# Third block of the key operand: copied on chip by ScalarE instead of loaded a third time

## The chip, the cores and the metric

The kernel runs on one core of a Trainium2 chip. The metric is the device time of one execution in microseconds; the time before is the median of three runs.

## The reference

A batch of 8 sequences of 224 rows of 512 features passes a cross attention over 750 context rows with 16 heads of 32 features, and then a feed-forward part that picks the 2 nearest of 32 prototypes for each row. Shortened:

```python
q, k, v = layernorm(x) @ w_q.T + b_q, ctx @ w_k.T + b_k, ctx @ w_v.T + b_v   # 16 heads of 32
scores = einsum('bthd,bshd->bhts', q * 32 ** -0.5, k) + bias[None]
scores = where(mask[:, None, None, :], NEG_INF, scores)
x = x + einsum('bhts,bshd->bthd', softmax(scores), v).reshape(8, 224, 512) @ w_o.T + b_o
y = layernorm(x)
w = softmax(-distance(y, prototypes) / t);  topw, topi = top_k(w, 2)         # topw made to sum to 1
x = x + sum over the two slots of topw * (A[topi] @ (B[topi] @ y) + bias[topi])
```

## The kernel before, in words

Everything is computed in 32-bit floats. To keep precision, a projection splits each operand in a high part (rounded to the fp32r format, in which TensorE multiplies) and a low part (the rest), and adds up three products: high by high, high by low, low by high.

The first stage (`weave`) does the attention. Its work is cut in 256 units: unit `w` is one head and one half of the 224 query rows of one batch. 32 units make a batch, 8 units a group of four heads (a group is numbered `n`, 0 to 31; four groups make a batch). While TensorE does the units of batch b, it also does the projections of batch b+1 in small shares between the steps of a unit (`project_steps`). In the last batch, units 224 to 255, there is nothing left to project. Before unit 0 the projections of batch 0 run alone.

Projected keys and queries go from the chip to memory (`k_parts`, `q_parts`, each with a high and a low part) and come back in another layout (`load_keys`, line 351). For one group there are four heads side by side in the free dimension, and in the partitions 97 rows: three blocks of 32 features, and a row with the mask (against a row of ones). With `k_st` as the moving operand and `q_st` as the weights, one product over 97 rows gives all three partial products and the mask at once. The blocks are key high, key low, key high, against query high, query high, query low. So the third key block is the same data as the first: it is loaded from memory twice. `k_st` and `q_st` are double buffered by the group's parity.

What the engines do in one unit:

- TensorE, `turn(w, 0)`: three transposes of probabilities (line 867), which wait for the Exp of unit w and for VectorE's copy of the unit before; then some projection steps, `score(w + 2)` (lines 854 and 858), some more, `turn(w, 1)`, and the rest. After every fourth unit comes `weigh` (line 885), the product with the values `v_sb`, and after every eighth the transposes of the sums (line 894).
- VectorE: the addition of the bias with the row maximum (line 696), the copy of half of the transposed probabilities (line 706), the low parts of projection tiles (lines 639, 646, 652) and, once a group, the product `attn` (line 720).
- ScalarE: the Exp of unit w+1 (line 574), the high parts of projection tiles (lines 553, 561, 568), the copy of the other half of the probabilities (line 583) and, once a group in its third unit, `sums_out` (line 589), which releases line 720.

Each engine works off its own list, written out by hand, in order; a wait holds up all that stands behind it. In the fourth unit of batches 1 to 6 TensorE's transposes also wait for line 720 of the group before (line 914), as the transposes of the next batch's `x` use the same bank.

SyncE issues the transfers, also in order: the stores of finished projection tiles (`store_tile`), the key load of group n+2 in the seventh unit of group n (line 425), the value load of a group in its second unit (line 427, line 376), and the context loads in halves. In the last batch GpSimd issues the loads of the weights for the second stage (line 481). Value tiles use two buffers: a tile waits for the store of the one two before.

The second stage (`finish`) begins after the last unit, about 770 us into the span. It does the output projection and the feed-forward part.

Of the kernel before, what the change touches and what calls it, by code (L numbers as in the profile page):

```python
# [8 lines left out]
F32 = mybir.dt.float32  # L9
# [3 lines left out]
ACT = mybir.ActivationFunctionType  # L13
AX = mybir.AxisListType

P = 128
B, T, E = 8, 224, 512
S = 750
H, D = 16, 32
NP, RK = 32, 16  # L20
KT = E // P
HG = P // D
NG = H // HG
# [6 lines left out]
UG = HG * TC  # L30
# [48 lines left out]
UNITS = B * UB  # L79
# [58 lines left out]
def ended(b, u, *pieces):  # L138

    if b >= B or u < 0:  # L140
        return []
    cuts, ends = CUTS[b][u], tile_ends(b)
    return [n for n in range(NT) for p in pieces if cuts[p] < ends[n] <= cuts[p + 1]]
# [54 lines left out]
def weave(nc, x, ctx_t, bias, mask, w_in_t, b_in, bv, b_out, scratch, attn_t, w_dram, sh):  # L198


    with ExitStack() as ctx:
# [3 lines left out]
        def sem(name):  # L205
            return ctx.enter_context(nc.semaphore(name))
# [95 lines left out]
        exp_done = sem("exp_done")  # L302
        prob_ready = [sem(f"prob_ready{j}") for j in range(2)]
        prob_copied = [sem(f"prob_copied{j}") for j in range(2)]
        weigh_done = sem("weigh_done")
        rsum_ready = sem("rsum_ready")
        rsum_wide_ready = sem("rsum_wide_ready")
# [12 lines left out]
        def _(eng):  # L320
# [30 lines left out]
            def load_keys(n):  # L351
                b, g = divmod(n, NG)
                p = g % 2
                if n >= 2:
                    eng.wait_ge(score_ready, UG * (n - 1))
                eng.wait_ge(k_stored[g], 64 * (b + 1))
                eng.wait_ge(q_stored[g // 2], 32 * (b + 1))
                if g < 2:
                    eng.dma_start(k_st[p][MROW:MROW + 1, :, :].bitcast(F32),
                                  scratch["mask"][b:b + 1, :].unsqueeze(1).broadcast_to([1, HG, S]))\  # L360
                       .then_inc(kq_loaded[p], 16)
                for j in range(NBLK):
                    eng.dma_start(k_st[p][j * D:(j + 1) * D, :, :].bitcast(F32),
                                  scratch["k"][b, (0, 1, 0)[j], g * P:(g + 1) * P, :]
                                  .rearrange("(r d) s -> d r s", d=D)).then_inc(kq_loaded[p], 16)
                    eng.dma_start(q_st[p][j * D:(j + 1) * D, :, :].bitcast(F32),
                                  scratch["q"][b, (0, 0, 1)[j], g * P:(g + 1) * P, :]
                                  .rearrange("(r d) t -> d r t", d=D)).then_inc(kq_loaded[p], 16)
# [174 lines left out]
        def _(eng):  # L543
# [28 lines left out]
            def exp(w):  # L572
                eng.wait_ge(added, w + 1)
                nc.scalar.activation(scores[:, w % NSC, :], scores[:, w % NSC, :], ACT.Exp,  # L574
                                     bias=neg_max[:, w % UB:w % UB + 1], scale=-1.0,
                                     accum_out=sums[:, w % UB:w % UB + 1]).then_inc(exp_done, 1)

            def copy(w):
                q, h = divmod(w, HG)
                if h == 0 and q >= 2:  # L580
# [3 lines left out]
                                     prob_ps[1][0:SW, 0:BT * TW].rearrange("p (s t) -> p s t", s=BT),  # L584
                                     ACT.Copy).then_inc(prob_copied[1], 1)

            def sums_out(n):
                eng.wait_ge(out_ready, n + 1)
                nc.scalar.activation(rsum_t[:, :], out_ps[:, 256:256 + T], ACT.Copy).then_inc(rsum_t_ready, 1)
# [21 lines left out]
                    nc.scalar.activation(w_hi[2][:, k, :], w_stage[2][:, k, :], ACT.Copy).then_inc(wv_hi_ready, 1)  # L611
            eng.wait_ge(wk_ready, KT)
            eng.wait_ge(wv_ready, KT)
            exp(0)
            for w in range(UNITS + 3):
                b, u = divmod(w, UB)
                if w + 1 < UNITS:
                    exp(w + 1)
                for n in ended(b + 1, u - 1, 2) + ended(b + 1, u, 0):
                    high_tile(b + 1, n)  # L620
                if b + 1 < B and u in X_AT:
                    high_x(b + 1, X_AT.index(u), out_ps)
                if w < UNITS:
                    copy(w)
                for n in ended(b + 1, u, 1):
                    high_tile(b + 1, n)
                if u % UG == 2 and w > UG:
                    sums_out(w // UG - 1)
# [160 lines left out]
        def _(eng):  # L789
# [53 lines left out]
            def score(w):  # L843
                n, h, c = w // UG, w % HG, w // HG % TC
                b, g = divmod(n, NG)
                p = n % 2
                if w % UG == 0:
                    eng.wait_ge(kq_loaded[p], 208 * b + 16 + 96 * (g // 2 + 1))
                at = 786 * (w % 2)
                main = (0, 512) if w % 2 == 0 else (S - 512, S)  # L850
                mid = (512, S) if w % 2 == 0 else (0, S - 512)
                if w >= 2:
                    eng.wait_ge(added, w - 1)
                nc.tensor.matmul(score_ps[:, at + main[0]:at + main[1]], q_st[p][:, h, c * TW:(c + 1) * TW],  # L854
                                 k_st[p][:, h, main[0]:main[1]], start=True, stop=True)
                if w >= 1:
                    eng.wait_ge(added, w)
                nc.tensor.matmul(score_ps[:, at + mid[0]:at + mid[1]], q_st[p][:, h, c * TW:(c + 1) * TW],  # L858
                                 k_st[p][:, h, mid[0]:mid[1]], start=True, stop=True).then_inc(score_ready, 1)
# [659 lines left out]
```

## Time and profile before

| | |
|---|---|
| median of 3 runs | 972.43 us (969.31 to 973.49) |
| profiled execution | 967.28 us |
| its span | 965.6 us |
| TensorE products busy | 873.9 us, 91% |
| VectorE busy | 616.2 us, 64% |
| ScalarE busy | 499.7 us, 52% |
| DMA | 144.35 MB, mean 149 GB/s |
| key loads | 96 transfers of 375 KB |

The span is the time from the first to the last instruction that the profiler sees. The percentages are shares of the span, over stages with different limits; so the table says which engine is loaded most, not what is worth how much. PE stands for TensorE's products, PEld for its weight loads, DVE for VectorE, ACT for ScalarE, POOL for GpSimd, SPq for the transfers that SyncE issues.

### The profile page before, as it was taken

Reading aid. Unit: us, or ns where it says so; the run is one execution under the profiler, and the core shown is the slowest. Engines: PE = TensorE matmul, PEld = TensorE weight load, DVE = VectorE, ACT = ScalarE, POOL = GpSimd, SP = SyncE. Lnnn points to the kernel's source line nnn. Section 1 sums busy time; section 2 is a strip of 40 time slices with the busy share of each in tenths; the row PEclk is TensorE's granted clock in tenths of the full one; section 3 lists DMA queues with packets and bytes.
Section 4 is the critical chain, followed back from the end, with each engine's and each line's share of the span. In section 5 each row is a group of like instructions: output and inputs, shape, how many; then the busy total and the mean of one; then the engine's idle time right before and its main releaser. Section 6 shows DMA issues by size and latency. Waiting matters only on the chain. (4 is left out here: it accounts for less than half of the span.)

```text
span 965.6 us, 21000 instructions
## 1 busy us (share of the span) xinstructions
PE 873.9 (91%) x8016; PEld 761.5 (79%) x8016; DVE 616.2 (64%) x1452; ACT 499.7 (52%) x1061; POOL 199.1 (21%) x245
## 2 busy tenths in 40 slices
PE   7577999999999999999999999999948868999996
PEld 6556897898789888978988898889747648888884
DVE  5425677667666766776686667666637556666662
ACT  4204565655556555656655665556537625334441
POOL 2241011212100210112021002110146222234300
PEclk9778999999999999999999999999979979999999
DMA  7585675977577576758775675576585311112201
GB/s 246 177 196 163 169 204 127 216 191 192 125 191 219 147 166 179 203 137 207 189 195 128 184 214 151 144 194 181 132 176 151 93 49 39 57 57 67 67 20 38
DMA packets 107803, 144.35 MB, mean 149 GB/s; under 512 B 8869, under 2 KB 83149, under 8 KB 107714
## 3 DMA queue, kind: packets, MB, share of 16 engines
q1 hardware_dynamic: 105218, 134.49, 54.0%
q0 software_dynamic: 2496, 8.65, 3.1%
q8 instruction: 59, 0.97, 0.5%
q14 instruction: 30, 0.25, 0.1%
HBM read 91.54 MB, written 51.57 MB: 148 GB/s over the span
## 5 line engine op out<-in xcount | busy, mean ns | idle before, releaser
L574 ACT ACTIVATE score_sb<-score_sb,neg_max 112x750 f32<-112x750 f32 x256 | 235.9, 921 | 108.7 <-DVE neg_max L696 107.9
L696 DVE CUSTOM_DVE_ANT_0 score_sb<-score_ps,neg_bias 112x750 f32<-112x750 f32 x256 | 239.4, 935 | 63.5 <-PE score_ps L858 61.8
L867 PE MATMUL prob_ps<-ident,score_sb 112*125 112x112 f32 x1536 | 254.5, 275 | 18.6 <-ACT score_sb L574 8.2
L867 PEld LDWEIGHTS prob_ps<-ident,score_sb 112*125 112x125 f32 x1536 | 226.0, 188 | 51.5 <-issue 13.5
L706 DVE COPY probs_sb<-prob_ps 125x336 f32<-125x336 f32 x256 | 129.6, 506 | 132.6 <-PE prob_ps L867 130.4
L583 ACT ACTIVATE probs_sb<-prob_ps 125x336 f32<-125x336 f32 x256 | 114.8, 448 | 191.9 <-PE prob_ps L867 190.4
L473 POOL COPY rsum_wide<-rsum 112x256 f32<-112x256 f32 x32 | 12.7, 397 | 472.3 <-DVE rsum L715 472.3
L854 PE MATMUL score_ps<-k_st,q_st 97*112 97x512 f32 x256 | 108.2, 423 | 0.0
L813 PE MATMUL acc<-ctx_hi,w_hi 128*128 128x376 f32 (+1 forms) x256 | 92.9, 363 | 14.5 <-DVE k_lo L639 7.8
L885 PE MATMUL out_ps<-probs_sb,v_sb 125*32 125x112 f32 x3072 | 88.0, 263 | 12.7 <-DMA v_sb<-v_all 12.1
L813 PE MATMUL acc<-ctx_hi,w_lo 128*128 128x376 f32 (+1 forms) x256 | 91.0, 355 | 0.0
L885 PEld LDWEIGHTS out_ps<-probs_sb,v_sb 125*32 125x32 f32 x3072 | 72.4, 111 | 23.2 <-DMA v_sb<-v_all 12.4
L813 PE MATMUL acc<-ctx_lo,w_hi 128*128 128x376 f32 (+1 forms) x256 | 90.6, 354 | 0.0
L821 PE MATMUL acc<-w_hi,ctx_hi 128*125 128x512 f32 x192 | 81.6, 425 | 6.6 <-DVE v_out L646 6.6
L858 PE MATMUL score_ps<-k_st,q_st 97*112 97x238 f32 x256 | 72.8, 284 | 10.6 <-DVE neg_max L696 9.9
L821 PE MATMUL acc<-w_hi,ctx_lo 128*125 128x512 f32 x192 | 81.2, 423 | 0.0
L821 PE MATMUL acc<-w_lo,ctx_hi 128*125 128x512 f32 x192 | 79.5, 414 | 0.0
L813 PEld LDWEIGHTS acc<-ctx_hi,w_hi 128*128 128x128 f32 x256 | 49.9, 195 | 18.0 <-DVE k_lo L639 8.3
L858 PEld LDWEIGHTS score_ps<-k_st,q_st 97*112 97x112 f32 x256 | 45.5, 178 | 22.6 <-DVE neg_max L696 18.1
L466 POOL TENSOR_TENSOR ctx_lo<-ctx_raw,ctx_hi 128x376 fp32r<-128x376 f32 x56 | 55.5, 992 | 4.7
L813 PEld LDWEIGHTS acc<-ctx_lo,w_hi 128*128 128x128 f32 x256 | 50.1, 196 | 1.3
L813 PEld LDWEIGHTS acc<-ctx_hi,w_lo 128*128 128x128 f32 x256 | 49.8, 195 | 1.2
(159 smaller groups left out, 1504.0 us busy)
## 6 DMA issues: line engine op xcount, KB each, us to landing
k_st<-k_parts SPq DMA_DIRECT2D x96, 375.0 KB
v_all<-v_out SPq DMA_DIRECT2D x48, 250.0 KB
v_sb<-v_all SPq DMA_DIRECT2D x32, 375.0 KB
q_st<-q_parts SPq DMA_DIRECT2D x96, 112.0 KB
ctx_raw<-in_ctx_t SPq DMA_DIRECT2D x14, 752.0 KB, 7.9
k_parts<-k_hi SPq DMA_DIRECT2D x32, 188.0 KB, 2.4
k_parts<-k_lo SPq DMA_DIRECT2D x32, 188.0 KB, 4.9
k_parts<-k_hi SPq DMA_DIRECT2D x32, 187.0 KB, 3.1
```

The lines of the kernel that those rows point to most:

```text
L466: eng.tensor_tensor(ctx_lo[f][:, k, :], src, ctx_hi[f][:, k, :].bitcast(F32), ALU.subtract)\
L473: eng.tensor_copy(rsum_wide[:, :, :, :], rsum[:, :].rearrange("t (c r) -> t c r", c=TC).unsqueeze(3) .broadcast_to([TW, TC, HG, D])).then_ ...
L574: nc.scalar.activation(scores[:, w % NSC, :], scores[:, w % NSC, :], ACT.Exp, bias=neg_max[:, w % UB:w % UB + 1], scale=-1.0, accum_out=su ...
L583: nc.scalar.activation(probs_sb[q % 2][0:SW, h * ST + BT:(h + 1) * ST, :], prob_ps[1][0:SW, 0:BT * TW].rearrange("p (s t) -> p s t", s=BT) ...
L696: nc.vector.tensor_tensor_reduce(out=scores[:, w % NSC, :], in0=score_ps[:, at:at + S], in1=neg_bias[:, w // HG % TC, :], scale=1.0, scala ...
L706: nc.vector.tensor_copy(probs_sb[q % 2][0:SW, h * ST:h * ST + BT, :], prob_ps[0][0:SW, 0:BT * TW].rearrange("p (s t) -> p s t", s=BT))\
L813: last = nc.tensor.matmul(acc[n % 2][:, 0:SH[f]], w_part[a][1][:, k, g * P:(g + 1) * P], ctx_part[c][f][:, k, K_AT[f]:K_AT[f] + SH[f]], st ...
L821: last = nc.tensor.matmul(acc[n % 2][0:SW, :], ctx_part[c][f][:, k, at:at + SW], w_part[a][2][:, k, :], start=(r == 0), stop=(m == end - 1))
L854: nc.tensor.matmul(score_ps[:, at + main[0]:at + main[1]], q_st[p][:, h, c * TW:(c + 1) * TW], k_st[p][:, h, main[0]:main[1]], start=True, ...
L858: nc.tensor.matmul(score_ps[:, at + mid[0]:at + mid[1]], q_st[p][:, h, c * TW:(c + 1) * TW], k_st[p][:, h, mid[0]:mid[1]], start=True, sto ...
L867: last = nc.tensor.transpose(prob_ps[j][0:SW, s * TW:(s + 1) * TW], scores[:, w % NSC, (BT * j + s) * SW:(BT * j + s + 1) * SW], ident[0:T ...
L885: last = nc.tensor.matmul(out_ps[h * D:(h + 1) * D, c * TW:(c + 1) * TW], v_g[p][:, s, h * D:(h + 1) * D], probs_sb[q % 2][0:SW, h * ST + ...
```

## The change

The third key block is no longer loaded. SyncE issues only the loads of blocks 0 and 1 (the three loads of `q_st` stay), so the counts that are waited for go from 96 to 80 a group pair. ScalarE copies block 0 to block 2, one head at a time: 32 partitions by 750 elements, 128 copies in all. The first copy of a group waits for the group's whole key load. The four copies of group n stand in the third to sixth unit of group n-1, each right behind the copy of line 583 and ahead of `sums_out`. Those of groups 0 and 1 stand ahead of the first Exp. The first score product of a group waits for the load and for its four copies.

```diff
+        k_copied = sem("k_copied")
...
                 for j in range(NBLK):
-                    eng.dma_start(k_st[p][j * D:(j + 1) * D, :, :].bitcast(F32),
-                                  scratch["k"][b, (0, 1, 0)[j], g * P:(g + 1) * P, :]
-                                  .rearrange("(r d) s -> d r s", d=D)).then_inc(kq_loaded[p], 16)
+                    if j < 2:
+                        eng.dma_start(k_st[p][j * D:(j + 1) * D, :, :].bitcast(F32),
+                                      scratch["k"][b, j, g * P:(g + 1) * P, :]
+                                      .rearrange("(r d) s -> d r s", d=D)).then_inc(kq_loaded[p], 16)
...
+            def copy_keys(n, h):
+
+                b, g = divmod(n, NG)
+                p = g % 2
+                if h == 0:
+                    eng.wait_ge(kq_loaded[p], 176 * b + 16 + 80 * (g // 2 + 1))
+                nc.scalar.activation(k_st[p][2 * D:3 * D, h, :], k_st[p][0:D, h, :].bitcast(F32), ACT.Copy)\
+                    .then_inc(k_copied, 1)
...
             eng.wait_ge(wv_ready, KT)
+            for n in range(2):
+                for h in range(HG):
+                    copy_keys(n, h)
             exp(0)
...
                 if w < UNITS:
                     copy(w)
+                if 2 <= u % UG < 2 + HG and UG < w < UNITS - UG:
+                    copy_keys(w // UG + 1, u % UG - 2)
...
                 if w % UG == 0:
-                    eng.wait_ge(kq_loaded[p], 208 * b + 16 + 96 * (g // 2 + 1))
+                    eng.wait_ge(kq_loaded[p], 176 * b + 16 + 80 * (g // 2 + 1))
+                    eng.wait_ge(k_copied, HG * (n + 1))
```

## Rows read from the trace of the kernel before

**Rows 1.** The page's first part: busy time, share and instructions of each engine.

```profile
PE 873.9 (91%) x8016; PEld 761.5 (79%) x8016; DVE 616.2 (64%) x1452; ACT 499.7 (52%) x1061; POOL 199.1 (21%) x245
```

**Rows 2.** Windows: stretch and length, busy of each engine, granted clock, DMA share, GB/s.

```profile
61.00:79.00 18.00, 8.96 (x27) 6.80 (x27) 6.02 (x11) 0.00 (x0) 4.80 (x7) 0.69 0.63 148
168.00:181.00 13.00, 12.07 (x123) 10.94 (x122) 7.51 (x19) 8.41 (x18) 4.79 (x7) 1.00 1.04 221
457.50:480.00 22.50, 22.50 (x240) 20.32 (x239) 14.81 (x34) 13.27 (x29) 2.85 (x4) 1.00 0.72 180
706.00:718.00 12.00, 0.84 (x15) 0.66 (x17) 1.06 (x3) 1.85 (x5) 5.33 (x7) 0.59 1.02 198
725.00:739.60 14.60, 13.11 (x162) 10.51 (x162) 11.51 (x27) 11.30 (x28) 11.61 (x15) 1.00 0.53 136
```

**Rows 3.** Waits from 90 to 700 us: total, times, longest, in us.

```profile
PE prob_ps L867 <- DVE attn L720: 3.6, 6, 0.6
```

**Rows 4.** Timeline of the start: start, duration, instruction, idle before it and releaser.

```profile
75.26 0.69 DVE L646 TENSOR_TENSOR v_out<-acc,bv_row 125x512 f32<-125x512 f32 x1 [7.55 <-DMA v_all<-v_out]
79.21 0.54 PE L858 MATMUL score_ps<-k_st,q_st 97*112 97x238 f32 x1 [5.88 <-DVE neg_max L696]
79.28 0.92 ACT L574 ACTIVATE score_sb<-score_sb,neg_max 112x750 f32<-112x750 f32 x1 [31.93 <-DVE neg_max L696]
```

**Rows 5.** Timeline around 717 us: the value load's issue and the product behind it.

```profile
699.46 0.27 SPq L376 DMA_DIRECT2D v_sb<-v_all  x1
...
717.45 2.47 PE L885 MATMUL out_ps<-probs_sb,v_sb 125*32 125x112 f32 x48 [11.16 <-DMA v_sb<-v_all]
```

**Rows 6.** ScalarE's groups by shape: busy us, mean ns, idle before.

```profile
L574 ACT ACTIVATE score_sb<-score_sb,neg_max 112x750 f32<-112x750 f32 x256 | 235.9, 921 | 108.7 <-DVE neg_max L696 107.9
L593 ACT ACTIVATE w_hi<-probs_sb 128x512 fp32r<-128x512 f32 x4 | 2.5, 630 | 3.1 <-DMA probs_sb<-in_w_in_t 3.0
L595 ACT ACTIVATE ctx_hi<-ctx_raw 128x376 fp32r<-128x376 f32 x4 | 2.1, 514 | 0.1
```

**Rows 7.** Timeline of ScalarE, VectorE and TensorE around 176 and 185 us.

```profile
175.31 0.45 ACT L583 ACTIVATE probs_sb<-prob_ps 125x336 f32<-125x336 f32 x1 [0.70 <-PE prob_ps L867]
175.66 0.35 ACT L589 ACTIVATE rsum_t<-out_ps 128x224 f32<-128x224 f32 x1
176.15 0.38 DVE L720 TENSOR_TENSOR attn<-out_ps,rsum_t 128x224 f32<-128x224 f32 x1
176.58 0.58 PE L867 MATMUL prob_ps<-ident,score_sb 112*125 112x112 f32 x3 [0.60 <-DVE attn L720]
184.62 0.44 ACT L583 ACTIVATE probs_sb<-prob_ps 125x336 f32<-125x336 f32 x1
186.81 0.40 PE L854 MATMUL score_ps<-k_st,q_st 97*112 97x512 f32 x1
```

**Rows 8.** The page's last part: issues with their count and size.

```profile
k_st<-k_parts SPq DMA_DIRECT2D x96, 375.0 KB
v_all<-v_out SPq DMA_DIRECT2D x48, 250.0 KB
...
q_st<-q_parts SPq DMA_DIRECT2D x96, 112.0 KB
```

**Rows 9.** Timeline of SyncE's issues: start and duration of the issue.

```profile
65.88 12.71 SPq L342 DMA_DIRECT2D v_all<-v_out  x4
...
166.08 0.64 SPq L359 DMA_DIRECT2D k_st<-mask_rows  x1
```

**Rows 10.** ScalarE's idle times in one group of the last batch.

```profile
731.57 0.92 ACT L574 ACTIVATE score_sb<-score_sb,neg_max 112x750 f32<-112x750 f32 x1 [0.30 <-DVE neg_max L696]
...
733.09 0.92 ACT L574 ACTIVATE score_sb<-score_sb,neg_max 112x750 f32<-112x750 f32 x1 [0.17 <-DVE neg_max L696]
...
734.69 0.92 ACT L574 ACTIVATE score_sb<-score_sb,neg_max 112x750 f32<-112x750 f32 x1 [0.25 <-DVE neg_max L696]
...
736.37 0.45 ACT L583 ACTIVATE probs_sb<-prob_ps 125x336 f32<-125x336 f32 x1 [0.67 <-PE prob_ps L867]
```

## The prediction

> **What bounds the kernel.** I read the page's totals first: TensorE is busy 873.9 us of 965.6, ScalarE 499.7 [rows 1]. Then the windows: in the long stretch in which one batch's attention is woven with the next batch's projections (about 79 to 694 us), a window such as 457.5 to 480 has TensorE busy all of its 22.5 us with ScalarE busy 13.27; the last batch, which has nothing to project, looks otherwise: in 14.6 us TensorE has 13.1 and ScalarE 11.3 [rows 2]. So whatever makes TensorE wait in the long stretch is lost one for one, and ScalarE work there is free as long as nothing on TensorE waits for it; in the last batch a ScalarE delay soon shows. Third, TensorE's waits: from 90 to 700 us they are small, among them six of 0.6 us each for `attn`, line 720 [rows 3]. Outside that stretch, two stalls come from DMA: at the start (61 to 79 us, TensorE busy 8.96 of 18 at a mean granted clock of 0.69), and 11.16 us for `v_sb` at 717.45 [rows 2, 4, 5]. The change takes from DMA and adds to ScalarE, so it must be priced at these places; the average load of either says nothing.
>
> **Price of one added copy.** 128 instructions of 32 x 750. ScalarE's time goes by the elements of a partition: 128x376 takes 0.514 us and 128x512 0.630 us, both from SBUF [rows 6], so 0.85 ns per element, and 750 give 0.83 us. An Exp of 750 elements takes 0.921 [rows 6], the upper end; the 512-element 0.63 is the lower. In a queue with no gap the next instruction starts 0.1 us before the end of the one before (175.31 plus 0.45, next at 175.66) [rows 7], so each copy moves what is behind it by 0.73 us (0.53 to 0.92).
>
> The Trainium skill ("ScalarE: Activation LUTs", rules for kernel authors) budgets about 0.3 us an instruction and 0.83 ns an element, 0.92 us here; the rows are nearer to 0.83. By the page's 0.92 and the same overlap, the terms on ScalarE's path below would grow by an eighth to a quarter, 1.3 us in all, which changes no conclusion.
>
> **Price of one removed load.** 375 KB [rows 8], that is 0.384 MB. While a key load, a value load and a context load run together, DMA's share is 1.04 and it moves 221 GB/s [rows 2], so 1.74 us of all DMA engines. I take 1.8 (1.2 to 2.2; the lower end if its share goes by packets, one transfer of six in a load of some 8 us). SyncE also issues 32 transfers fewer, which nothing waits for.
>
> **Start: -3.6 us.** All is DMA here. VectorE's value tile at 75.26 waits 7.55 us for a store; the bias addition of unit 0 stands behind it and the next tile, and TensorE waits 5.88 us for that, until 79.21 [rows 4]. The stores stand in SP's queue behind the key loads of groups 0 and 1 [rows 4, 9], so each load that loses a block brings them 1.8 us forward. What comes late next: eight copies ahead of the first Exp. Those of group 0 fall in a time in which ScalarE does nothing (0.00 us busy from 61 to 79) [rows 2]. Those of group 1 wait for its load, which lands before the store behind it, so before 75.26, and by 71.6 after; four copies end near 75, when the first addition is done too. Range -2.4 to -6: the addition may come no earlier than the copies let the Exp run, or the shorter stall may keep the clock up (the granted mean from 61 to 79 is 0.69) [rows 2].
>
> **Copies in the long stretch: +4.4 us, and 0.6.** Of 27 groups with four copies each there, the order decides. In the third to sixth unit of a group of eight, the copy sits between the probabilities' copy (line 583) and what follows. Units last about 2.7 us and ScalarE is busy 13.3 of 22.5, so it has 1.1 us idle a unit [rows 2]: most copies disappear there. The exception is the third unit. There the new copy stands ahead of `sums_out` (line 589, at 175.66), which releases the product on VectorE (line 720, 176.15 plus 0.38), which releases TensorE at 176.58 after 0.60 us of waiting [rows 7]. At the first group of batches 1 to 6 TensorE takes its next transposes into the same bank and already waits there; nothing stands between. 6 x 0.73 = 4.4 us (0 to 5.5). Besides, in each of these six places the copy first waits for its key load. It is issued from 166.08 on, behind a value store of 250 KB [rows 8, 9]. Its six transfers (three of 375 KB, three of 112) are 1.50 MB; with that store, at 221 GB/s [rows 2], they take 7.9 us from 168, so 175.9, less 1.8 without the block: 174.1, and ScalarE comes at 175.66. I put 0.1 us on each, 0.6 (0 to 12: up to 2 us each, if the load shares DMA with what is issued after it). Last, the score product of the new group (line 854, 186.81) waits for its fourth copy. ScalarE's copy of that unit is at 184.62 [rows 7]; 0.35 and 0.83 behind it, and up to 0.73 of lag from the third, put the end at 185.8 to 186.5. Close, but taken as 0 (0 to 0.2 us for 27 groups).
>
> **`v_sb` at 717.45: -1.8 us.** This load was issued at 699.46, right behind group 29's key load; DMA is full until it lands (share 1.02 from 706 to 718) [rows 2, 5]. One block fewer ahead of it: 1.8 us (0 to 4; the key load of group 30 and the weight loads from GpSimd's queue compete with it). The four copies of group 29 come here too, and any wait of theirs is covered by what is left of the 11.2 us.
>
> The Trainium skill ("SBUF — State Buffer", "Door 1: The DMA port swizzle") says that rows 0 to 63 use one set of eight DMA ports and rows 64 to 127 the other. The removed block fills rows 64 to 95, so it is the one that doesn't share its ports with the other two; were ports the limit, its removal would free nothing, which is the first rival below. The same page ("Can I just issue two DMAs to hit both halves?") says that two such transfers serialize nevertheless, and by that 1.8 us stands.
>
> **Last batch: +3.0 us.** Groups 30 and 31. Over the four units that get copies, up to the probabilities' copy at 736.37, ScalarE is idle 0.30, 0.17, 0.25 and 0.67 us, 1.4 in all [rows 10]. Four copies bring 4 x 0.73 = 2.9; 1.5 is left over, and TensorE waits for it through the Exp. Two groups: 3.0 (0, if the 3.3 us of idle in 14.6 [rows 2] take it all, to 5.8, none of it).
>
> **Sum.** -3.6 + 4.4 + 0.6 - 1.8 + 3.0 = +2.6 us. The profiled execution took 967.28 us (span 965.6), the median of the runs is 972.43, 5.15 above it; the same difference on the median gives 975.0.
>
> **Rivals.**
> 1. *ScalarE waits for the load* (slower). Place: third unit of the first group of batches 1 to 6. If the removed block frees nothing for the other two, each load lands at 175.9 or later against 175.66, and what ScalarE waits goes through lines 589 and 720 to TensorE one for one. For it: a share of 1.04 with several transfers in flight [rows 2] hides which of them lands when. Against: the same rows show DMA as the thing shared. It decides from a landing later than 175.7. Price, with 1 us each, no relief at `v_sb`, and that of the start kept: 4.4 + 6 + 3.0 - 3.6 = +9.8, 982.
> 2. *ScalarE becomes the bound beyond this*: the fourth copy of a group is late by 0.2 us 27 times (+5.4) and the last batch hides nothing (+2.8). 2.6 + 8.2 = +10.8, 983. For it: 0.3 us of room before 186.81 [rows 7]. Against: 1.1 us idle a unit.
> 3. *DMA relief is worth more* (faster). Start -6 with the clock kept up, `v_sb` -4, last batch +1: -6 + 4.4 - 4 + 1 = -4.6, 968. For it: two stalls of 5.9 and 11.2 us that only DMA sets. Against: both are long, and most of each is other traffic.
>
> **How the numbers follow.** Forecast 975.0 with chance 0.5, rival 1 0.2, rival 2 0.13, rival 3 0.17. Over 0.5% (4.9 us) is what a measurement of this kernel can tell; the runs before spread from 969.31 to 973.49. The forecast lies within it, though its upper terms reach past 977.3: of its 0.5, 0.08 is slower and 0.02 faster. Rivals 1 and 2 are slower, save 0.03; rival 3 is faster by more than 0.5% in 0.12 of its 0.17. So faster 0.14, same 0.48, slower 0.38. Range 967 to 984: both sides' rivals are inside it, their tails out.
>
> **What would show it.** 128 copies of about 0.83 us on ScalarE; the first Exp near 75.7 in place of 79.28 [rows 4]; six waits of TensorE for line 720 grown from 0.6 to 1.3 us; the `v_sb` wait, counted from the landing, 1.8 us earlier; TensorE's waits for the Exp larger in the last batch alone. It is wrong if TensorE waits in the long stretch for `k_st`, if ScalarE's copies wait long for DMA, or if the start gains nothing.

## The result: 1% slower

The changed kernel takes 980.09 us (median of 5 runs, 978.98 to 981.26); the kernel before, run beside it, 972.43 (969.02 to 973.69). The ratio over the runs is 1.0098, 95% interval 1.0073 to 1.0123; the two medians alone give 1.0079. Predicted were 975.0 and most likely "no change". The range holds the time; the likeliest case does not. Two executions among all runs below, one of the GpSimd copies (980.46 us) and one of key 30 waits (1587.49 us), were slow ones and are in no median, range or ratio.

The profiled executions stand at 979.36 (span 977.7) and 967.28 (span 965.6), 12.1 us apart, while the medians are 7.7 apart. Before's profiled run is a quick one of its kind; in its other runs the mean granted clock of TensorE goes from 0.968 (about 967 to 970 us) down to 0.961 (about 973). After's was an ordinary one, 0.7 us under its median. So the 5.15 us that the prediction added to its sum covered part of what the sum lacked: against its own trace the sum (+2.6) is 9.5 us short. The ledger below is made between the two traces, and has to account for 12.

The totals and the new rows of the changed kernel's page follow. The last two rows are a group of instructions (busy us, mean ns, idle before it) and the issues of the key load:

```profile
PE 887.5 (91%) x8016; PEld 770.1 (79%) x8016; DVE 615.2 (63%) x1452; ACT 611.2 (63%) x1189; POOL 199.5 (20%) x245
...
L595 ACT ACTIVATE k_st<-k_st 32x750 fp32r<-32x750 f32 x128 | 105.4, 828 | 28.3 <-DMA q_st<-q_parts 25.5
...
k_st<-k_parts SPq DMA_DIRECT2D x64, 375.0 KB
```

The 128 copies cost 0.828 us each, as priced, and ScalarE went from 499.7 us [rows 1] to 611.2; it is still far from being the bound. TensorE has the same 8016 matmuls and is "busy" 13.6 us longer: part of the loss shows as slower matmuls, not as waiting.

**Where the time went.** For each unit of attention (256 in all; batch b begins at unit 32b) I took the start of its first transpose in both traces and subtracted. All numbers are in us, and minus is earlier than before. Each row is one profiled execution. The long stretch is units 1 to 224, "v_sb" is 224 to 231, and the last batch is 231 to 255. "Long" in the prediction is 4.4 + 0.6.

```
                     start   long   v_sb   last batch   shift at unit 255
predicted            -3.6    +5.0   -1.8   +3.0         +2.6
changed kernel       -2.6   +15.5   -6.9   +6.0        +12.0
relief alone         -3.3    +1.8  -10.0   +0.1        -11.5
copies alone         +0.2   +37.6   -5.0   +7.8        +40.7
sums first           -1.8    +3.5   -7.8   +7.9         +1.8
sums first, again    -2.6    +3.5   -7.6   +7.1         +0.4
two at third         -2.7   +31.5   -6.1   +9.0        +31.8
tail loaded          -4.3    +3.4   -6.7    0.0         -7.6
tail loaded, again   -3.6    +3.5   -6.8    0.0         -6.9
three groups         -2.8    +0.3   -8.1    0.0        -10.6
key 30 waits         -0.3    +0.1   -5.8   +0.1         -5.9
start and wait       -1.3    +1.9   -5.3   +0.6         -4.2
GpSimd copies        -3.7   +11.0  -11.6   +8.7         +4.4
GpSimd in pieces     -2.4    -4.9  -10.3   +7.5        -10.1
```

**The long stretch.** The waits of the changed kernel, 90 to 700 us (total, times, longest):

```profile
DVE attn L736 <- ACT rsum_t L600: 36.5, 27, 1.9
PE prob_ps L884 <- DVE attn L736: 12.3, 6, 2.6
ACT k_st L595 <- DMA q_st<-q_parts: 3.5, 6, 1.1
PEld score_ps L871 <- issue: 3.5, 13, 0.3
```

The second line answers to [rows 3]: the six waits for `attn` grew from 3.6 us to 12.3. One of them, in the timeline at 264 us (start, duration, instruction, idle before it):

```profile
262.77 0.45 ACT L585 ACTIVATE probs_sb<-prob_ps 125x336 f32<-125x336 f32 x1 [0.70 <-PE prob_ps L884]
...
263.84 0.83 ACT L595 ACTIVATE k_st<-k_st 32x750 fp32r<-32x750 f32 x1 [0.61 <-DMA q_st<-q_parts]
...
264.69 0.36 ACT L600 ACTIVATE rsum_t<-out_ps 128x224 f32<-128x224 f32 x1
...
265.08 0.39 DVE L736 TENSOR_TENSOR attn<-out_ps,rsum_t 128x224 f32<-128x224 f32 x1 [1.39 <-ACT rsum_t L600]
...
265.53 0.58 PE L884 MATMUL prob_ps<-ident,score_sb 112*125 112x112 f32 x3 [2.09 <-DVE attn L736]
```

ScalarE waits 0.61 us for the key load, copies, and only 0.85 us after the copy's start comes `sums_out`; 0.60 + 0.61 + 0.85 is 2.06, and TensorE waited 2.09. The same holds in all six places: ScalarE's waits there are 0.35, 0.61, 0.43, 1.09, 0.33 and 0.67, together 3.5, and 3.6 + 3.5 + 6 x 0.85 = 12.2. What comes after such a wait, in windows (length, busy of PE, PEld, DVE, ACT, POOL, granted clock, DMA share, GB/s):

```profile
262.00:265.40 3.40, 1.44 (x10) 1.13 (x8) 1.79 (x4) 2.06 (x5) 0.00 (x0) 1.00 0.96 255
266.30:269.50 3.20, 3.20 (x13) 3.07 (x13) 1.46 (x4) 0.54 (x1) 0.00 (x0) 0.50 0.41 147
270.00:273.00 3.00, 3.00 (x23) 2.94 (x22) 1.93 (x3) 2.93 (x6) 0.00 (x0) 1.00 0.03 9
```

TensorE's granted clock falls to 0.50 for 3.4 us, the lower of its two levels, although TensorE has no gap in it: 13 matmuls where the next 3 us hold 23. This happened behind three of the six waits (at 266, 447 and 539 us, behind waits of 2.09, 2.56 and 1.80), not behind those of 1.82, 1.90 and 2.14. The three batches with it lost 3.0, 3.8 and 2.7 us, the three without 1.75, 1.8 and 2.2. In the ledger's units right behind the wait a slow stretch costs 1.0, 1.3 and 1.0 us, 3.3 in all.

The rest is regular: 0.27 us at the eighth unit of batches 1 to 6, 1.6 in all, and 0.24 at the 23rd and 24th unit of batches 0 to 6, 1.7. Both are the same wait, the fourth line of waits: its 13 times are these 6 and 7. Each stands at TensorE's weight load for the first score product of a group, and each ends 0.07 us after that group's fourth copy. The first one of the second kind, with the copy that it waits for:

```profile
137.82 0.83 ACT L595 ACTIVATE k_st<-k_st 32x750 fp32r<-32x750 f32 x1
...
138.71 0.17 PEld L871 LDWEIGHTS score_ps<-k_st,q_st 97*112 97x112 f32 x1 [0.25 <-issue]
```

Sum: 8.7 + 3.3 + 1.6 + 1.7 = 15.3, for 15.5.

**`v_sb`.** The changed kernel where before has its 11.16 us wait [rows 5]:

```profile
712.48 0.27 SPq L378 DMA_DIRECT2D v_sb<-v_all  x1
...
717.40 0.83 ACT L595 ACTIVATE k_st<-k_st 32x750 fp32r<-32x750 f32 x1 [2.44 <-DMA q_st<-q_parts]
...
719.59 0.55 PE L884 MATMUL prob_ps<-ident,score_sb 112*125 112x112 f32 x3 [3.61 <-ACT score_sb L576]
...
723.42 0.30 SPq L365 DMA_DIRECT2D k_st<-k_parts  x1
...
723.94 2.47 PE L902 MATMUL out_ps<-probs_sb,v_sb 125*32 125x112 f32 x48
```

TensorE waits for `v_sb` no more. In its place it waits 3.61 us for the Exp, because ScalarE waits 2.44 for the key load of group 29 ahead of its copy. The net is -6.9, where -1.8 was predicted. The key load of group 30 is issued 10.9 us behind the value load, not 6.5 as before. The last part of the value load lands 9.7 us after its issue, where before it took 17.95 (the landing events on the semaphore that line 902 waits for). The experiments show what each is worth.

**Last batch.** The waits for the Exp from 715 to 775 us are 10.5 us in 14; before had 4.8 in 14 from 702 to 775. In group 30:

```profile
737.93 0.55 PE L884 MATMUL prob_ps<-ident,score_sb 112*125 112x112 f32 x3 [1.19 <-ACT score_sb L576]
...
740.13 0.58 PE L884 MATMUL prob_ps<-ident,score_sb 112*125 112x112 f32 x3 [0.76 <-ACT score_sb L576]
```

```profile
735.00:739.00 4.00, 2.76 (x18) 1.86 (x16) 3.02 (x8) 3.67 (x7) 3.50 (x5) 1.00 0.49 97
740.60:744.00 3.40, 3.40 (x55) 2.99 (x53) 1.46 (x3) 3.32 (x6) 3.23 (x4) 0.51 0.75 198
757.70:761.10 3.40, 3.40 (x36) 3.08 (x40) 1.46 (x3) 3.26 (x6) 0.00 (x0) 0.50 0.79 260
```

Each of the two groups loses 0.82 and 0.56 us in two units, 1.4 in all, and then 1.59 in the unit of a stretch at half clock, which before does not have there.

### The profile page after: what moved, and what is told of

Same layout as the page of the kernel before. It is cut to its first block and busy times, and to the rows that moved or that the text cites. A ratio compares the mean times of both kernels' runs of the same rounds, so it can differ in the third digit from the quotient of the medians.

```text
span 977.7 us, 21096 instructions
## 1 busy us (share of the span) xinstructions
PE 887.5 (91%) x8016; PEld 770.1 (79%) x8016; DVE 615.2 (63%) x1452; ACT 611.2 (63%) x1189; POOL 199.5 (20%) x245
## 5 line engine op out<-in xcount | busy, mean ns | idle before, releaser
L884 PE MATMUL prob_ps<-ident,score_sb 112*125 112x112 f32 x1536 | 257.4, 277 | 32.0 <-ACT score_sb L576 13.8
L884 PEld LDWEIGHTS prob_ps<-ident,score_sb 112*125 112x125 f32 x1536 | 229.2, 191 | 65.2 <-ACT score_sb L576 19.6
L595 ACT ACTIVATE k_st<-k_st 32x750 fp32r<-32x750 f32 x128 | 105.4, 828 | 28.3 <-DMA q_st<-q_parts 25.5
L902 PEld LDWEIGHTS out_ps<-probs_sb,v_sb 125*32 125x32 f32 x3072 | 74.0, 112 | 12.3 <-issue 6.1
L655 DVE SCALAR_TENSOR_TENSOR k_lo<-acc,bias_col,k_hi 128x376 fp32r<-128x376 f32 (+1 forms) x64 | 38.8, 606 | 26.9 <-ACT k_hi L555 26.9
```

Of the source, the lines that this page charges most:

```text
L595: nc.scalar.activation(k_st[p][2 * D:3 * D, h, :], k_st[p][0:D, h, :].bitcast(F32), ACT.Copy)\
L884: last = nc.tensor.transpose(prob_ps[j][0:SW, s * TW:(s + 1) * TW], scores[:, w % NSC, (BT * j + s) * SW:(BT * j + s + 1) * SW], ident[0:T ...
L902: last = nc.tensor.matmul(out_ps[h * D:(h + 1) * D, c * TW:(c + 1) * TW], v_g[p][:, s, h * D:(h + 1) * D], probs_sb[q % 2][0:SW, h * ST + ...
```

## The experiments

Times are medians; before's beside each set was 971.44, 969.24 or 971.98. Labels in the ledger's words.

**Relief alone, copies alone, order, engine.** Four kernels on one chip.

*Relief alone*: two loads, no copies past group 1. Groups 2 to 31 multiply with what block 2 still holds, so that part of the computation is left out.

```diff
-                if 2 <= u % UG < 2 + HG and UG < w < UNITS - UG:
-                    copy_keys(w // UG + 1, u % UG - 2)
...
-                    eng.wait_ge(k_copied, HG * (n + 1))
+                    eng.wait_ge(k_copied, HG * min(2, n + 1))
```

> The third key block is not loaded, and only groups 0 and 1 get copies; groups 2 to 31 multiply with what block 2 still holds (that part of the computation is left out). So this is the relief of DMA alone. Theory (the change's cost is all ScalarE's copies): start 2.6 us earlier as in the changed kernel, no TensorE wait for line 720 above the 0.6 us of before, and the wait for v_sb shorter by 1.8 us: 967 to 969 us, 4 to 6 below before. Rival (the removed block frees nothing behind the start): 970 us, v_sb wait still 11 us. Second rival (most of the v_sb wait is the queue of key loads): wait under 5 us, 962 to 964 us.

Measured 958.39 (957.6 to 963.59), ratio 0.9881 (0.9849 to 0.9913): lower than every case named; nearest is the second rival, whose wait of under 5 us came out as 0.41. By the ledger the start gives 3.3 us, the long stretch nothing (its +1.8 is mostly one stretch of TensorE at half clock, 1.6 us at unit 129), and `v_sb` 10.0:

```profile
697.97 0.27 SPq L378 DMA_DIRECT2D v_sb<-v_all  x1
...
707.06 0.30 SPq L365 DMA_DIRECT2D k_st<-k_parts  x1
...
707.75 1.36 PE L900 MATMUL out_ps<-probs_sb,v_sb 125*32 125x112 f32 x48 [0.41 <-DMA v_sb<-v_all]
```

The value load is used 9.8 us after its issue, against 18.0 before, though only 1.8 us of traffic (the prediction's price) was removed from ahead of it. The half clock of the long stretch, in a window as above:

```profile
428.80:432.20 3.40, 3.40 (x15) 3.27 (x13) 1.64 (x6) 1.01 (x2) 2.09 (x4) 0.50 0.95 221
```

TensorE had waited 0.57 and 0.36 us just before. It waits 0.57 and 0.37 in the same units of the kernel before, at 430.73 and 431.77, and keeps the full clock there.

*Copies alone*: the third load stays, and the copy overwrites what it brought.

```diff
-                    if j < 2:
-                        eng.dma_start(k_st[p][j * D:(j + 1) * D, :, :].bitcast(F32),
-                                      scratch["k"][b, j, g * P:(g + 1) * P, :]
+                    eng.dma_start(k_st[p][j * D:(j + 1) * D, :, :].bitcast(F32),
+                                  scratch["k"][b, (0, 1, 0)[j], g * P:(g + 1) * P, :]
...
```

> All three key blocks are loaded as before, and ScalarE's copies are made on top, in the changed kernel's places and waiting for the whole load: the cost of the copies alone, without relief. Theory (ScalarE's wait for the load and its copy both reach TensorE through lines sums_out and attn): the load lands about 1.8 us later than in the changed kernel, so six waits of TensorE for attn of about 4.3 us each in place of 2.05, plus the drop of the clock in all six batches, plus 6 us in the last batch: 20 to 30 us above before, 993 to 1002. Rival (the wait for the load is set by other traffic and the relief did nothing there): the six waits stay at 2 us, 982 to 986.

Measured 1008.74 (1007.6 to 1010.43), ratio 1.0384 (1.0363 to 1.0405): the theory's side, and above its range. Waits from 90 to 740 us:

```profile
PE prob_ps L883 <- DVE attn L735: 26.8, 6, 4.7
...
ACT k_st L594 <- DMA q_st<-q_parts: 18.3, 7, 3.3
```

The same path, with 2.4 us more in each wait, and all six followed by a slow stretch of TensorE. So the removed block did bring the load forward in the changed kernel. Where it is not removed, rival 1's mechanism is at work: ScalarE waits 2.4 to 3.3 us for the load at each of the six places.

*Sums first*: as the changed kernel, with the copy behind `sums_out`.

```diff
+                if u % UG == 2 and w > UG:
+                    sums_out(w // UG - 1)
                 if 2 <= u % UG < 2 + HG and UG < w < UNITS - UG:
                     copy_keys(w // UG + 1, u % UG - 2)
                 for n in ended(b + 1, u, 1):
                     high_tile(b + 1, n)
-                if u % UG == 2 and w > UG:
-                    sums_out(w // UG - 1)
```

> The changed kernel with one edit: in the third unit of a group sums_out stands ahead of the copy, not behind it. Theory (the cost in the long stretch is that order): the six waits for attn go back to 0.6 us (8.7 us less), the clock drops behind them go too (4 to 6 us less), the load's wait is hidden; 966 to 969 us, 11 to 14 below the changed kernel and a few below the kernel before. Rival (ScalarE's stall reaches TensorE anyway, through the Exp or the copy of line 585): only 0 to 5 us less than the changed kernel, 975 to 980.

Measured 967.95 (967.17 to 969.8), ratio 0.996 (0.9946 to 0.9974), as the theory said. Waits from 90 to 700 us:

```profile
PE prob_ps L884 <- DVE attn L736: 3.6, 6, 0.6
...
ACT k_st L595 <- DMA q_st<-q_parts: 2.3, 5, 0.9
```

The six waits are before's again [rows 3], no stretch at half clock is left between 90 and 700 us, and the long stretch costs 3.5 in place of 15.5: the two regular terms, 3.3, alone. ScalarE still waits 2.3 us for the loads and nobody notices. This shows the path: same copies, same loads, other order.

*GpSimd copies*: one 32x3000 copy for each group on GpSimd behind `widen`, none on ScalarE.

```diff
+                eng.tensor_scalar(k_st[p][2 * D:3 * D, :, :], k_st[p][0:D, :, :].bitcast(F32), 1.0, 0.0,
+                                  ALU.mult, ALU.add).then_inc(k_copied, 1)
...
```

> The third block is copied by GpSimd, one instruction of 32 x 3000 a group, behind its widening of the sums; ScalarE has no copies. Theory (GpSimd has 79% idle time and nothing of TensorE waits for it there): about as e1_no_copies, 962 to 968 us, last batch as before. Rival (GpSimd's copies hold up VectorE, or its context splits and weight splits come late): the copies take over 4 us each, VectorE's instructions grow or TensorE waits for k_st or ctx; 972 us or more.

Measured 973.1 (963.25 to 976.7), ratio 1.0007 (0.9973 to 1.004): the theory fell. The rival held in time and in VectorE's longer instructions, though a copy takes 2.69 us and not over 4. GpSimd's copy and what VectorE does meanwhile, with TensorE behind it:

```profile
145.81 3.38 DVE L704 TENSOR_SCALAR x_in<-x_in,mv,nwt 112x512 f32<-112x512 f32 x2
146.21 2.69 POOL L483 TENSOR_SCALAR k_st<-k_st 32x3000 fp32r<-32x3000 f32 x1 [2.80 <-DMA q_st<-q_parts]
...
149.74 0.55 PE L885 MATMUL prob_ps<-ident,score_sb 112*125 112x112 f32 x3 [2.03 <-DVE probs_sb L723]
```

VectorE's normalisation, from SBUF to SBUF, takes 0.54 us before. Here four of the sixteen take 2.92 to 2.97 us, a little longer than GpSimd's copy, and the probabilities' copy behind them on VectorE is late for TensorE. The line of the normalisation over the whole run (shortest, median, longest ns), in the kernel before and in this one:

```profile
L687 DVE TENSOR_SCALAR x_in<-x_in,mv,nwt x16: 539/544/548, 30.7 to 591.1; 112x512 f32<-112x512 f32 x16
```

```profile
L704 DVE TENSOR_SCALAR x_in<-x_in,mv,nwt x16: 541/547/2967, 30.5 to 595.4; 112x512 f32<-112x512 f32 x16
```

The Trainium skill ("SBUF — State Buffer", "Who interferes with whom") says that VectorE in its two-port modes, which `tensor_scalar` can enter, and GpSimd share a pair of SBUF ports which one holds for its whole instruction while the other is blocked. The 2.97 us beside a 2.69 us copy agree with it. A second cost is of order again. In the last batch GpSimd's copy of group 29 waits 6.46 us for its load (until 711.64), the splits of the second stage's weights behind it come late, and a `rsum_wide` stands behind those at 728.82; TensorE waits 5.75 us for it at 729.29.

**The `v_sb` wait taken alone, the tail, and a larger dose.**

*Key 30 waits*: the kernel before, with the key load of group 30 issued only when the value load of group 28 has landed.

```diff
+                if n == B * NG - 2:
+                    eng.wait_ge(v_loaded[0], 16 * (2 * B - 1))
```

> The kernel before with one added wait: SyncE issues the key load of group 30 only when the value load of group 28 has landed. No load is removed. Theory (the 11.2-us wait for v_sb came from group 30's key load, issued while the value load was under way; the removed block helps because the value load then ends before that issue): the wait falls to 1 to 3 us, 961 to 964 us. Rival (the queue of group 29's key load ahead of it and GpSimd's weight loads set it): the wait stays above 8 us, 970 to 972.

Measured 966.06 (963.44 to 969.09), ratio 0.9974 (0.996 to 0.9987). That is between the two cases named, and 3.2 us under the median of before; the ledger's 5.9 is of the quickest of the eleven.

```profile
699.13 0.27 SPq L378 DMA_DIRECT2D v_sb<-v_all  x1
...
712.03 2.47 PE L887 MATMUL out_ps<-probs_sb,v_sb 125*32 125x112 f32 x48 [4.44 <-DMA v_sb<-v_all]
...
712.05 0.30 SPq L365 DMA_DIRECT2D k_st<-k_parts  x1
```

The value load now takes 12.9 us from issue to use, against 18.0: so a load that is issued behind it on the same queue, at 706.00 in before, had cost it 5.1. The wait is 4.4 us where I expected 1 to 3, so the block of group 29 ahead of it is worth more than 1.8 too: from 12.9 down to the 9.8 of relief alone is 3.1. The two together make the effect steep. A few us less ahead of the value load, and it is through when the next key load is issued.

The same count explains a line of the ledger that relief cannot: *copies alone* gains 5.0 at `v_sb` with every load kept. Its rows there:

```profile
737.24 0.27 SPq L377 DMA_DIRECT2D v_sb<-v_all  x1
...
744.84 0.83 ACT L594 ACTIVATE k_st<-k_st 32x750 fp32r<-32x750 f32 x1 [5.00 <-DMA q_st<-q_parts]
...
750.86 0.30 SPq L364 DMA_DIRECT2D k_st<-k_parts  x1
751.38 2.15 PE L901 MATMUL out_ps<-probs_sb,v_sb 125*32 125x112 f32 x48
```

The copy of group 29 holds TensorE up, the key load of group 30, which waits for TensorE, is issued 13.6 us behind the value load, and that one is used 14.1 us after its issue with no wait.

The landing events give the same without the use. The last part of the value load lands 17.95 us after its issue in the kernel before. It lands after 12.8 to 12.9 where the group ahead has its three blocks and nothing of group 30 is issued before the landing (key 30 waits, start and wait, copies alone). It lands after 9.6 to 9.7 in all kernels with two blocks ahead, the GpSimd ones apart. Of these, relief alone issues the key load 9.1 us behind the value load and the others 10.7 to 11.8. So in the changed kernel the gain is the missing block's. The hold that the copies put on TensorE adds nothing to it there, and takes 3.2 of it back (-6.9 against relief alone's -10.0). In the two GpSimd kernels the load lands after 7.7 us; there GpSimd, waiting for its own copy's load, issues none of its 256 KB weight loads meanwhile, where in the kernel before it issues three. So these loads count too; no run varies them alone.

*Tail loaded*: sums first, and groups 30 and 31 load their third block as before (the copies stop two groups sooner).

```diff
-                    if j < 2:
+                    if j < 2 or n >= B * NG - 2:
...
-                if 2 <= u % UG < 2 + HG and UG < w < UNITS - UG:
+                if 2 <= u % UG < 2 + HG and UG < w < UNITS - 3 * UG:
...
```

> The kernel of e3_sums_first, with the third block of groups 30 and 31 loaded from memory again instead of copied by ScalarE. Theory (ScalarE's four copies of a group cost 3 us each time in the last batch): 5 to 7 us less than e3_sums_first, 961 to 963 us. Rival (the key load of group 30 with its third block brings the wait for v_sb back, or the loads land late): 966 to 973.

Measured 961.09 (959.54 to 962.65), ratio 0.9923 (0.9906 to 0.9941), as expected; the last batch costs 0.0 in the ledger where sums first has 7 to 8 (and the changed kernel 6.0, with shorter stretches at half clock).

*Start and wait*: before, with the wait of key 30, and copies for groups 0 and 1 alone.

```diff
+                    if j < 2 or n >= 2:
...
+                if n == B * NG - 2:
+                    eng.wait_ge(v_loaded[0], 16 * (2 * B - 1))
...
```

> The kernel before with the wait of e5_key30_waits, and with the third block of groups 0 and 1 alone copied by ScalarE ahead of the first Exp; groups 2 to 31 load three blocks. Theory (these two places are the whole of DMA's relief): the start is 3 us earlier, the v_sb wait as in e5_key30_waits; 957 to 961 us, as fast as e1_no_copies or faster. Rival (fewer key loads also help in the long stretch): 3 or more us slower than e1_no_copies.

Measured 961.95 (960.12 to 964.05), ratio 0.9928 (0.9906 to 0.9949), just above the theory. Its median is 3.6 us over that of relief alone, which by number is the rival's side, but not by its mechanism: the long stretch is the same in both (+1.9 and +1.8), and the difference is at the start and at `v_sb`, where this kernel still loads the third block of group 29 (-5.3 for -10.0). The start gave 2.1 at the first unit, the least of all kernels. Another single stretch at half clock, 1.6 us, stands at unit 97. The GpSimd copies have three like it, at units 33, 129 and 161, and two at third, below, has one at 193. All six are at the second unit of a batch, where no edit put a new wait.

*Two at third*: the changed kernel with two copies ahead of `sums_out`.

```diff
-                if 2 <= u % UG < 2 + HG and UG < w < UNITS - UG:
-                    copy_keys(w // UG + 1, u % UG - 2)
+                if UG < w < UNITS - UG:
+                    for h in {2: (0, 1), 3: (2,), 4: (3,)}.get(u % UG, ()):
+                        copy_keys(w // UG + 1, h)
```

> The changed kernel with two copies instead of one in the third unit of a group (and one each in the fourth and fifth, none in the sixth): the price of what stands ahead of sums_out, by dose. Theory (each copy there reaches TensorE one for one, and a longer stall makes the clock drop more often): the six waits for attn grow by 0.73 us each, 4.4 in all, the clock drops in more of the six batches (up to 3.6 us more), the 0.27 us at each batch's eighth unit go (1.6 less); 984 to 989 us. Rival (only the wait for the key load counts, not the copy): 978 to 981.

Measured 997.72 (995.92 to 1000.15), ratio 1.0299 (1.0276 to 1.0322), above the theory.

```profile
PE prob_ps L885 <- DVE attn L737: 16.0, 6, 3.3
```

Of the +16.0 us in the long stretch over the changed kernel, 3.7 are the waits (I had 4.4). Stretches at half clock fill 24 us here against 10, and their units cost 8.8 against 3.3, 5.5 more. The rest is regular again: every batch from 0 to 6 loses 0.13 us at the 13th to 15th unit, 0.46 at the 21st to 23rd, 0.24 at the 29th and 0.43 at the 30th, where the changed kernel loses 0.24; that is 7.1 more, and 16.3 in all for 16.0. With it TensorE's weight loads for the transposes wait for the Exp 12.8 us in 33 places, against 4.9 in 13. The dose acts through the path named, but two copies in one unit also delay the Exp elsewhere, and a wait ahead of `sums_out` costs more than its length.

**Only where it helps, and the two repairs timed again.**

*Three groups*: groups 0, 1 and 29 copied on chip, behind `sums_out`; all others load three blocks.

```diff
+ON_CHIP = (0, 1, B * NG - 3)
...
+                    if j < 2 or n not in ON_CHIP:
...
+                if 2 <= u % UG < 2 + HG and w // UG + 1 == B * NG - 3:
+                    copy_keys(w // UG + 1, u % UG - 2)
...
```

> The kernel before, with only groups 0, 1 and 29 changed: two blocks loaded, the third copied by ScalarE (for group 29 behind sums_out). All other groups load three blocks; no added wait for group 30. Theory (DMA's relief is worth something at the start and ahead of v_sb, nowhere else): 3 us at the start, the v_sb wait gone for 2 to 3 us of ScalarE's wait; 957 to 960 us, 1 to 4 below e6_tail_loaded. Rival (the other groups' relief helps too): at or above e6_tail_loaded.

Measured 960.18 (958.18 to 962.9), ratio 0.9896 (0.9877 to 0.9914). With 12 copies in place of 128, start and `v_sb` are all there and the long stretch is flat (+0.3).

*GpSimd in pieces*: the GpSimd copy in four of 32x750.

```diff
-                eng.tensor_scalar(k_st[p][2 * D:3 * D, :, :], k_st[p][0:D, :, :].bitcast(F32), 1.0, 0.0,
-                                  ALU.mult, ALU.add).then_inc(k_copied, 1)
+                for h in range(HG):
+                    eng.tensor_scalar(k_st[p][2 * D:3 * D, h, :], k_st[p][0:D, h, :].bitcast(F32), 1.0, 0.0,
+                                      ALU.mult, ALU.add).then_inc(k_copied, 1)
```

> The kernel of e4_gpsimd with each group's copy in four instructions of 32 x 750 in place of one of 32 x 3000. Theory (VectorE's normalisation, SBUF to SBUF, stands still while GpSimd copies: 2.97 us in place of 0.54): it is held up by one piece of 0.7 us, and the 2-us waits of TensorE for VectorE's copy go; 3 to 6 us less than the 973 of e4_gpsimd, with its late widening at group 28 (5.8 us) still there. Rival (the instruction is slow for another reason): no change, 972 to 976.

Measured 959.13 (957.17 to 962.08), ratio 0.9888 (0.9868 to 0.9908): the right direction, and over twice the size.

```profile
L484 POOL TENSOR_SCALAR k_st<-k_st 32x750 fp32r<-32x750 f32 x128 | 105.5, 825 | 107.7 <-DMA q_st<-q_parts 99.6
```

```profile
L705 DVE TENSOR_SCALAR x_in<-x_in,mv,nwt x16: 537/546/1200, 31.3 to 584.7; 112x512 f32<-112x512 f32 x16
PE out_ps L913 <- POOL rsum_wide L475: 5.3, 1, 5.3
```

GpSimd spends more time than with one instruction a group (105.5 us for 86.2), but VectorE is held for less: a normalisation beside two of the pieces takes 1.05 us. The longest, 1.20, stands beside GpSimd's split of the context, not beside a copy; the changed kernel has one of 1.20 too. The 5.3 us behind `rsum_wide` stay, so there is room.

Its long stretch gains 4.9 us, and the traces show where: 0.45 to 0.84 us at the 27th and 28th unit of batches 0 to 5 (3.9 in all), and 1.0 in batch 6, where TensorE's 0.9 us wait for `v_sb` is gone. In the kernel before, VectorE's small steps ahead of the normalisation run beside GpSimd's split of the context:

```profile
148.59 0.50 POOL L464 TENSOR_SCALAR ctx_hi<-ctx_raw 128x376 fp32r<-128x376 f32 x1
...
148.69 0.42 DVE L677 TENSOR_TENSOR nwt<-rstd 112x2 f32<-112x2 f32 x1
...
149.18 0.99 POOL L466 TENSOR_TENSOR ctx_lo<-ctx_raw,ctx_hi 128x376 fp32r<-128x376 f32 x1
...
149.34 0.86 DVE L681 TENSOR_SCALAR nwt<-nwt 112x2 f32<-112x2 f32 x1
```

With GpSimd waiting for its key load, the split comes later and the same steps run alone:

```profile
146.35 0.16 DVE L695 TENSOR_TENSOR nwt<-rstd 112x2 f32<-112x2 f32 x1
...
146.74 0.17 DVE L699 TENSOR_SCALAR nwt<-nwt 112x2 f32<-112x2 f32 x1
```

So the kernel before has a loss of this kind of its own, about 1 us a batch on VectorE. The kernel with one copy a group gains the same 0.84 us in batches 1 and 4, where no normalisation is held. This is read from traces; no run moves the split alone.

*The two again*: tail loaded and sums first, side by side with three groups.

> The kernel of e6_tail_loaded once more, on the chip of e9 to e12, for the difference to e9_three_groups and e12_sums_first_again: 960 to 963 us.

> The kernel of e3_sums_first once more on the same chip. Theory (four copies of ScalarE in a group of the last batch cost 3 to 4 us): 5 to 8 us above e11_tail_loaded_again. Rival: under 3 us above it.

Measured 962.05 (960.05 to 963.21), ratio 0.9911 (0.9894 to 0.9928), and 968.34 (967.25 to 970.05), ratio 0.9973 (0.9961 to 0.9985). The tail is worth 6.3 us. Three groups is 1.9 under tail loaded, the side of the theory, though their ranges overlap. In the ledger the 108 copies between cost the two regular terms (+3.5 for +0.3 in the long stretch), and their relief gives nothing.

The quickest two are three groups and GpSimd in pieces, 1.0 and 1.1% under the kernel before and 2% under the changed one.

## Why the prediction was right in kind and short in size

- **Price of a copy: right.** 0.828 us for 0.83. The step in the queue was taken as 0.73, from an overlap of 0.1 that other rows show; ahead of `sums_out` it is 0.85, 0.7 us over six places. The budget of the Trainium skill ("ScalarE: Activation LUTs", rules for kernel authors) that gave 0.92 is for an instruction whose bias is a pointer operand. The Exp here has one and takes 0.921 us; the copy has none.
- **Start: right.** -3.3 at the first Exp (75.97 for 79.28 [rows 4], foreseen near 75.7), -2.6 one unit later. Over the eleven kernels with this edit the first unit came 2.1 to 4.3 us sooner, so this term has an uncertainty of its own.
- **Copies ahead of `sums_out`: the path right, the size short by 3.7.** The waits cost 8.7 us for 5.0. The load made 3.5 for 0.6: I worked out a landing 1.5 us ahead of need and put 0.1 us on each place; the six were 0.33 to 1.09. A landing worked out from a mean of GB/s is not good to 1 us. Rival 1 was the same mechanism at 1 us a place, and it came to a little over half of that.
- **The clock behind a wait: missing.** The prediction named the clock at the start only. Three slow stretches, 3.3 us, are there with the waits and gone with them in sums first; one in each group of the last batch, 1.6 each, takes 3.2 more. In us this is the largest miss, 6.5.
- **The fourth copy before the score product: missed.** "Close, but taken as 0"; it was 0.27 us six times and 0.24 seven times, 3.3 together. All kernels with one ScalarE copy a unit pay it, relief alone and three groups do not. The range given, up to 0.2 us a group, was too low where it struck, and 14 of the 27 groups pay nothing.
- **Last batch: the copies' term right.** 2 x 1.4 for 3.0; the other 3.2 are the clock.
- **`v_sb`: the step whose reasoning failed most.** I priced one block fewer at 1.8 us, as if the load were a sum of traffic. It gained 10.0 in relief alone and 6.9 net here. One block less ahead is worth 3.2 us (12.9 to 9.7 from issue to landing), and it lets the value load land with little or nothing of the key load of group 30 issued, which is worth 5.1 more. I also took any wait of group 29's copy as covered; ScalarE's 2.44 us for its load reached TensorE, and 3.2 us of the gain went back.
- **Why the total was near: luck in part.** The long stretch was short by 10.5 and the last batch by 3.0, the start by 1.0; `v_sb` gave back 5.1 more; the sum, short by 9.4 against the trace, was lifted by 5.15 of offset, of which the changed kernel's median had only 0.7. The 0.38 on slower was too little with three costs at their lower ends.
- **Rivals.** Rival 2's lateness of the fourth copy was real in 13 places, not 27, and ScalarE is no bound. Rival 3 was right that relief at `v_sb` is worth more, which relief alone shows; the copies outweigh it.

Open: why a load issued later on the same queue slows the one ahead of it (only that it does is shown); why only some of the waits are followed by the half clock, and why it also comes at the second unit of a batch without a new wait; what moving GpSimd's split of the context away from VectorE's steps would give by itself.

## What to carry to other kernels

Before putting work in an idle engine's queue, look at what stands right behind it: an instruction that releases the bound engine makes the whole delay, its wait for data included, reach that engine, and the clock added nearly four tenths of it again here. Moving such work behind the release cost nothing and gave 12 us here. Take load off the DMA only where the bound engine waits for a transfer; there, ask also which transfer is issued behind it and whether the one waited for now ends first, as that can be worth more than the bytes.

## What the runs showed of the hardware beyond this

- TensorE's granted clock fell to 0.50 inside work without a gap behind three of six waits of 1.8 to 2.6 us (changed kernel), five of six of 2.2 to 3.3 (two at third) and six of six of 3.9 to 4.8 (copies alone). It fell behind none of the six of 0.6 us for `attn` in sums first, but once each in relief alone and start and wait behind waits of 0.6 and 0.4 us.
- A value load of the same size landed 17.95, 12.9, 9.7 and 7.7 us after its issue, by what was issued ahead of it, behind it and by GpSimd.
- VectorE's steps on 112x2 elements took 0.16 and 0.17 us alone and 0.42 and 0.86 beside GpSimd's 128x376 instructions.
- GpSimd copies 32x750 fp32 in 825 ns and ScalarE in 828: the choice between them is one of order and of VectorE's instructions, not of speed.
